# Four groups of a three-layer interaction network split into a rounded part and a difference, and one more bank of sixteen scaled on ScalarE

## The reference

```python
h = x
outs = []
for W in (W0, W1, W2):
    h = einsum('bid,bjd,ijn->bnd', x, h, W.reshape(64, h.shape[1], 128))
    outs.append(h)
z = sum(concatenate(outs, axis=1), axis=-1)          # 512 x 384
h = relu(concatenate([z, dense_ctx], 1) @ W_top1 + b_top1)
h = relu(h @ W_top2 + b_top2)
y = h @ W_top3                                       # 512 x 1, float32
```

## Time and profile before

| | |
|---|---|
| time, median of 3 runs | 1166.59 us (1166.09 to 1166.8) |
| the profiled execution | 1167.73 us |
| its span, first to last instruction | 1165.9 us |
| PE busy | 1125.9 us, 97% |
| DVE busy | 879.1 us, 75% |
| POOL busy | 763.6 us, 65% |
| ACT busy | 562.2 us, 48% |
| granted TensorE clock, mean | 0.99 |

### The profile page before, as it was taken

One profiled execution on the slowest core, in us unless ns is written; L12 is line 12 of the kernel. 1 busy time (PEld: TensorE's weight loads), 2 busy tenths in 40 slices (PEclk: granted clock), 3 DMA queues, 4 the chain that ended last, 5 costly groups with the idle time before them and its releaser, 6 DMA issues.

```text
span 1165.9 us, 20547 instructions
## 1 busy us (share of the span) xinstructions
PE 1125.9 (97%) x4682; PEld 797.4 (68%) x4682; DVE 879.1 (75%) x2757; ACT 562.2 (48%) x1815; POOL 763.6 (65%) x660
## 2 busy tenths in 40 slices
PE   3899999999999999999999999999999999999999
PEld 2676666766677666667667666666667776667765
DVE  2787878887865778888786587888786588878830
ACT  3244545455543455455553355545554354555631
POOL 6686868768683675868685485877768268545630
PEclk9899999999999999999999999999999999999989
DMA  7574443331436224243442434233243621513000
GB/s 265 126 196 95 100 92 76 62 93 35 111 89 163 60 38 103 58 91 81 92 112 62 111 82 92 76 80 74 37 117 80 163 74 31 122 60 120 1 1 1
DMA packets 127789, 102.69 MB, mean 88 GB/s; under 512 B 77457, under 2 KB 86865, under 8 KB 127026
## 3 DMA queue, kind: packets, MB, share of 16 engines
q1 hardware_dynamic: 117522, 92.79, 32.0%
q0 software_dynamic: 8192, 2.11, 2.0%
q10 hardware_dynamic: 1952, 6.40, 1.4%
HBM read 97.06 MB, written 4.20 MB: 87 GB/s over the span
## 4 chain that ended last, share of the span: by engine, by line
PE 86%; DVE 5%; issue 4%; DMA 2%; POOL 2%; ACT 0%; DVEq 0%; SPq 0%; POOLq 0%; ACTq 0%
PE tps L789 19%; PE acc L747 19%; PE tps L791 18%; PE tps L790 18%; PE side L816 5%; DVE parts_sb L546 3%; PE side L803 2%; PE acc L743 1%; PE side L811 1%; PE tps L881 1%; POOL rows_sb L470 1%; DVE z_sb L516 1%; DMA roll_sb<-x_halves 1%; PE side L763 1%; DVE parts_sb L542 0%
## 5 line engine op out<-in xcount | busy, mean ns | idle before, releaser
L546 DVE SCALAR_TENSOR_TENSOR parts_sb<-tps,xcol_sb,parts_sb 128x128 f32<-128x128 f32 x2432 | 671.8, 343 | 194.1 <-PE tps L791 187.6
L634 ACT ACTIVATE y_sb<-tps,xcol_sb 128x128 f32<-128x128 f32 x1536 | 439.6, 370 | 526.9 <-PE tps L791 526.8
L789 PE MATMUL tps<-w_hi_sb,h_hi_sb 128*128 128x512 f32 x1024 | 511.7, 500 | 13.0 <-DVE parts_sb L546 9.7
L790 PE MATMUL tps<-w_lo_sb,h_hi_sb 128*128 128x512 f32 x1024 | 404.6, 395 | 0.0
L791 PE MATMUL tps<-w_hi_sb,h_lo_sb 128*128 128x512 f32 x1024 | 404.3, 395 | 0.0
L789 PEld LDWEIGHTS tps<-w_hi_sb,h_hi_sb 128*128 128x128 f32 x1024 | 192.4, 188 | 131.5 <-issue 46.4
L408 POOL DMA_INDIRECT rows_sb<-tables,rows_now_sb x240 | 230.4, 960 | 71.6 <-issue 43.7
L747 PE MATMUL acc<-prod_sb,w_sb 128*128 128x512 f32 (+1 forms) x544 | 269.4, 584 | 4.6 <-DVE prod_sb L499 4.5
L423 POOL TENSOR_TENSOR ysum_sb<-y_sb 128x1024 f32<-128x1024 f32 x64 | 153.8, 2403 | 172.5 <-ACT y_sb L634 171.8
L790 PEld LDWEIGHTS tps<-w_lo_sb,h_hi_sb 128*128 128x128 f32 x1024 | 192.8, 188 | 87.7 <-issue 57.3
L791 PEld LDWEIGHTS tps<-w_hi_sb,h_lo_sb 128*128 128x128 f32 x1024 | 192.3, 188 | 46.9
(11 more groups left out here) (56 smaller groups left out, 366.7 us busy)
## 6 DMA issues: line engine op xcount, KB each, us to landing
roll_sb<-x_scratch SPq DMA_DIRECT2D x240, 256.0 KB
w_sb<-w_rows SPq DMA_DIRECT2D x40, 256.0 KB, 3.5
gsum_sb<-w_rows ACTq DMA_DIRECT2D x8, 512.0 KB, 9.1
roll_sb<-x_halves SPq DMA_DIRECT2D x32, 128.0 KB, 3.0
rows_sb<-tables,rows_now_sb POOLq DMA_INDIRECT x240
x_scratch<-rows_sb SPq DMA_DIRECT2D x30, 128.0 KB, 3.9
xx_sb<-x_scratch SPq DMA_DIRECT2D x15, 256.0 KB, 2.7
roll_sb<-x_scratch SPq DMA_DIRECT2D x30, 64.0 KB
```

The lines of the kernel that those rows point to most:

```text
L546: dve.scalar_tensor_tensor(part, bank, scale, part, ALU.mult, ALU.add).then_inc(d_done, 1)
L634: done = act.activation(y[:, pair % Y_RING, half * CH + u * NF:half * CH + (u + 1) * NF], tps[:, p % RING, u * NF:(u + 1) * NF], ACT.Copy, ...
L789: pe.matmul(bank, h1_hi[:, par, cols], w1_hi[:, of], start=True, stop=False, skip_group_check=True)
L790: pe.matmul(bank, h1_hi[:, par, cols], w1_lo[:, of], start=False, stop=False, skip_group_check=True)
```

## The change

Groups 1, 3, 5 and 7 of layer 0 (`SPLIT`) are split as layer 1 already is, for chunks 1 to 15: ScalarE rounds their product to `hi` (float32r, one buffer), VectorE writes the difference `lo` over the product, and TensorE does six float32r matmuls (four at the first place, two at the second) instead of two in float32. Their weights are split once at the start into `w0_hi` and `w0_lo`. Chunk 0 still uses the whole weights. On the other side ScalarE takes seven banks of a block instead of six, at k = 1, 3, 5, 8, 10, 12, 14; `y` is seven banks without a ring, and GpSimd adds the seventh with an instruction of its own.

```diff
-A_IN = (1, 3, 6, 8, 11, 13)
+A_IN = (1, 3, 5, 8, 10, 12, 14)
...
+SPLIT = (1, 3, 5, 7)
+HI_AT = tuple(L0_AT[g] - 6 for g in SPLIT)
+LO_AT = tuple(L0_AT[g] - 4 for g in SPLIT)
...
+def hi_at_places(q):
+    return tuple(FIRST_L0_AT[g] - 3 for g in SPLIT) if q < 0 else HI_AT
+def lo_at(q):
+    return tuple(FIRST_L0_AT[g] - 2 for g in SPLIT) if q < 0 else LO_AT
...
-        y = sb("y", [P, Y_RING, 2 * CH])
+        y = sb("y", [P, BLOCK_A, CH])
...
             def add_pairs(q, t, p):
...
+                if bank == 3:
+                    pool.wait_ge(a_done, here)
                     if q >= 0 or s > 0:
                         pool.wait_ge(h2t_ready, t * SUB + s)
+                    pool.tensor_tensor(whole, y[:, 0:2], y[:, 2:4], ALU.add).then_inc(y_step, 1)
+                if bank == 5:
+                    pool.wait_ge(a_done, here)
+                    pool.wait_ge(y_step, before + 1)
+                    pool.tensor_tensor(whole, whole, y[:, 4:6], ALU.add).then_inc(y_step, 1)
+                    pool.wait_ge(y_step, before + 2)
                     pool.tensor_tensor(ysum[:, 0:CH], ysum[:, 0:CH], ysum[:, CH:2 * CH], ALU.add).then_inc(y_step, 1)
+                if bank == 6:
+                    pool.wait_ge(a_done, here)
+                    pool.wait_ge(y_step, before + 3)
+                    pool.tensor_tensor(ysum[:, 0:CH], ysum[:, 0:CH], y[:, 6], ALU.add).then_inc(y_step, 1)
+                    pool.wait_ge(y_step, before + 4)
                     pool.tensor_tensor(ysum[:, 0:CH // 2], ysum[:, 0:CH // 2], ysum[:, CH // 2:CH], ALU.add).then_inc(y_step, 1)
...
+            def subtract(q, t, g):
+                slot = ring_place(q, g, 2)
+                dve.wait_ge(hi_ready, (t - 1) * len(SPLIT) + (SPLIT.index(g) + 1))
+                dve.tensor_tensor(lo[:, slot], prod[:, slot], hi[:].bitcast(F32), ALU.subtract).then_inc(lo_ready, 1)
...
+            dve.wait_ge(w0_hi_ready, 1)
+            dve.tensor_tensor(w0_lo[:], w0_whole[:], w0_hi[:].bitcast(F32), ALU.subtract).then_inc(w0_lo_ready, 1)
...
+            def round_hi(q, t, g):
+                act.wait_ge(prod_ready, t * GROUPS + (g + 1))
+                e = SPLIT.index(g)
+                if e > 0:
+                    act.wait_ge(prod_used, t * GROUPS + (SPLIT[e - 1] + 1))
+                else:
+                    act.wait_ge(prod_used, t * GROUPS + (SPLIT[-1] + 1 - GROUPS))
...
+                act.activation(hi[:], prod[:, ring_place(q, g, 2)], ACT.Copy).then_inc(hi_ready, 1)
...
             def scale_bank(q, t, p):
...
+                if bank % 2 == 0 and (s > 0 or q >= 0):
+                    taken = (1, 1, 2, 4)[bank // 2]
+                    act.wait_ge(y_step, t * (SUB * STEPS_OF_SUM) + ((s - 1) * STEPS_OF_SUM + taken))
...
+            def add_split(q, t, g, passes):
+                e, slot = SPLIT.index(g), ring_place(q, g, 2)
+                if 0 in passes:
...
+                    for i in range(2):
+                        pe.matmul(acc[:], w0_hi[:, 2 * e + i, :], hi[:, i, :], start=False, stop=False, skip_group_check=True)
+                        pe.matmul(acc[:], w0_lo[:, 2 * e + i, :], hi[:, i, :], start=False, stop=False, skip_group_check=True)
+                if 1 in passes:
+                    pe.wait_ge(lo_ready, (t - 1) * len(SPLIT) + (e + 1))
+                    for i in range(2):
+                        mm = pe.matmul(acc[:], w0_hi[:, 2 * e + i, :], lo[:, slot, i, :], start=False, stop=False,
+                                       skip_group_check=True)
+                    mm.then_inc(prod_used, 1)
```

More of the change, by code:

```diff
@@ L45 @@
 TILES0 = 2 * WHOLE
+SPLIT = (1, 3, 5, 7)
+RAW = tuple(g for g in range(WHOLE) if g not in SPLIT)
+SPLIT_TILES, RAW_TILES = 2 * len(SPLIT), 2 * len(RAW)
 ROLL = 4
@@ L143, in build @@
         w0_at = here()
-        w0 = sb("w0", [P, TILES0, NF])
+        w0 = sb("w0", [P, RAW_TILES, NF])
+        w0_hi = sb("w0_hi", [P, SPLIT_TILES, NF], F32R)
+        w0_lo = sb("w0_lo", [P, SPLIT_TILES, NF], F32R)
         w0_end = sb("w0_end", [FIELDS, NF])
@@ L159, in build @@
         prod_at = here()
-        prod = sb("prod", [P, 2, 2, CH])
+        sb("prod_space", [P, 2, 2, CH])
+        prod = over("prod", [P, 2, 2, CH], prod_at)
+        lo = over("lo", [P, 2, 2, CH], prod_at, F32R)
+        hi_at = here()
+        hi = sb("hi", [P, 2, CH], F32R)
         h1_hi = sb("h1_hi", [P, 2, CH], F32R)
@@ L174, in build @@
         w0_back = over("w0_back", [P, TILES0, NF], y_at)
+        w0_whole = over("w0_whole", [P, SPLIT_TILES, NF], hi_at)
         w1_whole = gsum[:].rearrange("p i b -> p (i b)")
@@ L618, in scale_bank @@
                 a = a_before(p)
-                pair, half = divmod(a, 2)
+                bank = a % BLOCK_A
                 if a == 0 and q < 0:
@@ L633, in scale_bank @@
                     i = QUAD * k + u
-                    done = act.activation(y[:, pair % Y_RING, half * CH + u * NF:half * CH + (u + 1) * NF],
+                    done = act.activation(y[:, bank, u * NF:(u + 1) * NF],
                                           tps[:, p % RING, u * NF:(u + 1) * NF], ACT.Copy,
@@ L679, in _ @@
                 round_w1(k)
+            act.wait_ge(w0_summed, 1)
+            act.activation(w0_hi[:], w0_whole[:], ACT.Copy).then_inc(w0_hi_ready, 1)
             act.wait_ge(consts_loaded, 48)
@@ L737, in layer0 @@
                         pe.wait_ge(first_z1, 1)
[L738 to L739 removed]
+                    if q > -2 and g in SPLIT:
+                        pe.wait_ge(hi_ready, (t - 1) * len(SPLIT) + (SPLIT.index(g) + 1))
+                    else:
+                        pe.wait_ge(prod_ready, t * GROUPS + (g + 1))
+                if q > -2 and g in SPLIT:
+                    add_split(q, t, g, tiles)
+                    return
+                add_group(g, ring_place(q, g, 2), HALVES[1] if q == -2 else slice(0, CH), tiles, prod_used)
+            def add_split(q, t, g, passes):
+                e, slot = SPLIT.index(g), ring_place(q, g, 2)
+                if 0 in passes:
+                    if q < 0 and e == 0:
+                        pe.wait_ge(w0_lo_ready, 1)
+                    for i in range(2):
[7 more added lines that the diff above has]
+                    mm.then_inc(prod_used, 1)
             def add_group(g, slot, cols, tiles, used):
@@ L746, in add_group @@
                 for i in tiles:
-                    mm = pe.matmul(acc[:, cols], w0[:, 2 * g + i, :], prod[:, slot, i, cols], start=g == 0 and i == 0, stop=False,
+                    weights = w0_whole[:, 2 * SPLIT.index(g) + i, :] if g in SPLIT else w0[:, 2 * RAW.index(g) + i, :]
+                    mm = pe.matmul(acc[:, cols], weights, prod[:, slot, i, cols], start=g == 0 and i == 0, stop=False,
                                    skip_group_check=True)
@@ L945 @@
     other = [np.concatenate([pairs0[turned[k], here] for k in (2 * n, 2 * n + 1)]) for n in range(TILES0)]
-    arrays["w0_tiles"] = np.ascontiguousarray(np.stack(there, 1))
-    arrays["w0_back"] = np.ascontiguousarray(np.stack(other, 1))
+    order = [2 * g + i for g in RAW + SPLIT for i in range(2)]
+    arrays["w0_tiles"] = np.ascontiguousarray(np.stack([there[n] for n in order], 1))
+    arrays["w0_back"] = np.ascontiguousarray(np.stack([other[n] for n in order], 1))
     arrays["w0_end"] = np.ascontiguousarray(pairs0[here, turned[2 * TILES0]])
```

50 lines of the change are left out of this document (23 added, 27 removed).

## The result

The changed kernel takes 1160.1 us (median of 7 runs, 1158.13 to 1163.79), the kernel before 1166.59 (7 runs on the same chip): a ratio of 0.9947, 95% interval 0.9935 to 0.9959. So it is faster by 6.5 us (6.2 by the ratio), where 22.0 were forecast. The profiled execution took 1162.44, with a span of 1160.6: 5.3 less than the span before, and 2.3 above its own median.

What follows compares the result with a forecast made beforehand. PE, busy 97% of the span, was taken as the bound; -17.9 - 5.6 + 0.8 + 0.7 = -22.0 us gave 1144.6 us from the median 1166.59, own range 1140 to 1149 (chance 0.58), 8-in-10 range 1140 to 1161.

Steps and rivals of the forecast that it cites:

- the lock term: DVE's subtraction of two SBUF operands beside POOL, at place 46: PE loses 0 to 24 us in all, taken as 0.
- Rival 1: DVE's subtractions held by POOL's additions, at place 46 or another: 1149 to 1161, 1155 in the middle; chance 0.20.
- rival 3: POOL's backlog delays block 1's first addition, so ACT waits at place 33 and PE at 37: 1173; chance 0.09.
- the others follow the loop's return and stay: Of PE's 17 waits for DVE, those not at a chunk's start or short ones with W2 stay unchanged.
- Float32r: Layer 0's split groups on PE: six float32r matmuls for two float32 tiles, -1.28 per chunk, -17.9 us in 14 chunks.
- The wait at a chunk's start: Place 0 comes 0.54 late for DVE; 0.44 goes in eleven chunks, with the three short waits -5.6 us.
- Cover: DVE's and ACT's changed work stays hidden behind PE if banks are taken within three places: 0.
- Rivals 2 and 4: Rival 2: wait at chunk's start stays, 1150, chance 0.09. Rival 4: matmuls into acc run at 0.28, 1162, chance 0.04.
- The three short waits in chunks with W2: PE's three waits of 0.25 for DVE in chunks with W2 go: 0.75 of the 5.6 us gain.
- The tail: At the end POOL reaches h2t later, with one more addition of 1.37 but starting 0.70 earlier: +0.7 us.
- The first chunk: Place 0 of the next chunk comes at 115.9 instead of 115.08: +0.8, bounds -1.3 and +2; +0.2 on the table's stretch.
- The start: One more DMA, ACT's rounding of w0_hi and DVE's w0_lo are covered: 0, at most +0.5.

Runs made afterwards that it cites:

- no_lock: The changed kernel with the subtraction lo = prod - hi replaced by lo = hi * xx, one operand in PSUM: 1150.83 us, ratio 0.9858.
- warm28: The changed kernel with 28 warming matmuls ahead of the loop instead of 20: 1157.30 us, ratio 0.9910.
- banks_only: The kernel before with ScalarE's seven banks, seven y and POOL's fifth addition, layer 0 left in raw float32: 1166.15 us, ratio 1.0001.
- no_lock_warm28: "Both out": the changed kernel with lo = hi * xx for the subtraction and 28 warming matmuls instead of 20: 1143.83 us, ratio 0.9795.
- split_only: The changed kernel with the kernel before's six ScalarE banks, ring of four pairs of y and four POOL additions: 1165.31 us, ratio 0.9990.
- lo7_earlier: The changed kernel with group 7's subtraction alone moved from place 46 to place 45: 1156.91 us, ratio 0.9916.
- unrolled: The changed kernel with its loop over three blocks written out on every engine: 1151.68 us, ratio 0.9872.

## Why the prediction was wrong

**The step that failed** is the lock term: "I take 0, the nearest row being L553 and the gathers being held." Its size is 10.4 us (no_lock), inside the bounds of 0 to 24 that stood beside it. Rival 1, at a chance of 0.20, is what happened, at its place (46, then PE at 51), with its sign in the trace; 1144.6 and 10.4 give 1155, its middle. That 1160.1 lies in its 1149 to 1161 as well is luck, since the loop's return, which it left out, is in that number. By stretch, the changed kernel's profile less no_lock's, place 51 makes 6.7 of it (1.1 in six chunks), the first chunk 2.6, one chunk in which ACT waits for a POOL that was held earlier 1.8, and the last interval 0.9.

Two things went wrong in choosing. The earlier trace rows have gathers only: one that comes up behind the subtraction and is held, and one, at 31.62, that is 0.70 under way when the subtraction starts and doesn't hold it. The case in dispute was an addition under way, and a row with a gather says nothing on that. (The hold of 0.9 that rival 3 calls measured is 0.54 there, 1.49 less 0.95.) And the count of times could not carry the choice: subtraction at 48.0 into the chunk, POOL's addition anywhere from 45.2 to 48.2 (three holds of 0.9 make 47.9). It came at 47.95 and the subtraction at 48.47 (chunk from 518.60): the addition was first by 0.52. With both orders open I should have priced the term in its middle. The Trainium skill, "SBUF — State Buffer", section "SBUF: two separate sides", had the rule that decided, and the trace agrees for additions: 2.96 for a start 0.52 into an addition of 2.40. For gathers it does not always: the one at 31.62 held nothing.

**A step missed**: "the others follow the loop's return and stay." They grew, by the second pause and the lower clock. Taking the second pause out gives 4.3 (warm28), and the two intervals then sum to 157.3, 2.4 less than before where 3.1 were forecast. Both out together give 17.7, the whole shortfall of 15.8 (22.0 less 6.2) and a little more; the sum of each alone is 14.7, and the 3.0 between is within what the intervals leave open.

**Right, by measurement.** Float32r: chunks go from 64.09 (banks_only) to 62.72 (no_lock), 1.37 for the forecast 1.28. The wait at a chunk's start: 64.68 to 64.09, 0.59 for 0.44. Together 1.96 a chunk for 1.72, which is why "both out" beats the forecast in the steady part. Cover: no new wait of PE in 62.73 us. Rivals 2 and 4 did not occur.

**Off in size.** The three short waits in chunks with W2 were to go, for 0.75; they stay, under "issue". The tail: PE's wait for h2t is 1.44 where it was 0.39, +1.05 for +0.7. The first chunk: +2.9 for +0.2, of which no_lock leaves +0.3 and no_lock_warm28 +1.2; the rest is held subtractions (PE waits 1.00 and 0.99 for lo) and held gathers ahead of the load of the earlier trace rows. The start is 1.3 to 2.6 faster in the kernels with the split, which was not forecast and not looked into. That place 0 behind the first chunk came at 115.86, where 115.9 was forecast, is chance: the start came 2.3 earlier, and the chunk took that much longer.

**Rival 3** was there in small: ACT waited 25.1 us for POOL's first addition, and PE saw 2.2 of it (1.65 at 494.34 and 0.57 at 972.47; the other 1.88 of its 4.1 for ACT is the first chunk's, where ACT waits for the load). It is a result of the exclusion, since ACT's wait falls to 6.0 without.

## What to carry to other kernels

Before an instruction of VectorE with both inputs in SBUF is set beside a busy GpSimd, price it with the other engine's longest instruction, at each place, for each phase; one operand in PSUM takes the price away (1.81 to 1.21 us on average here). An edit that adds or takes away instructions moves the code behind it: where a loop is jumped back to, time the kernel at two or three positions of that code before judging a change of half a per cent. A half of a change that measures as nothing may still work: look in its trace for a stretch without the loss (63.33 beside 64.65 in split_only) before saying what it needs.

## What the runs showed of the hardware

- An exclusion can cost more than one instruction: a subtraction that came up 0.41 into a gather lasted 4.02 in lo7_earlier, with POOL's addition behind the gather let through ahead of it. One that came up as far into a gather with another gather behind it was not held (1.22, at 395.63 in unrolled). One that comes up 0.02 into POOL's small h2t sum is not held (1.22), and the sum takes 1.56 for 0.46.
- The end of the kernel, from PE's last h2t matmul on, takes 40.1, 41.7 to 41.8, 43.4 to 43.5, or 45.1 us in the fourteen profiles, whatever the kernel, by how long the 1.2 GHz level lasts there. The windows from that matmul on, in no_lock and in no_lock_warm28:

```profile
1104.14:1109.14 5.00, 5.00 (x14) 0.67 0.00 0
1109.14:1114.14 5.00, 5.00 (x15) 0.50 0.00 0
1114.14:1119.14 5.00, 5.00 (x25) 0.50 0.00 0
1119.14:1124.14 5.00, 5.00 (x42) 0.97 0.01 3
```

```profile
1098.54:1103.54 5.00, 5.00 (x14) 0.69 0.00 0
1103.54:1108.54 5.00, 5.00 (x15) 0.50 0.00 0
1108.54:1113.54 5.00, 5.00 (x38) 0.79 0.01 3
1113.54:1118.54 5.00, 5.00 (x33) 1.00 0.00 0
```

  PE is busy in all of them; before them it had been idle 1.45 and 1.44 for h2t. The two ends differ by 1.70 us: a part of the scatter between profiled executions that no edit explains.
